# Three raw weight buffers, exchange DMAs ahead of the block's store, and raw loads issued by ScalarE, in the attention stage of a fused block

## The chip, the cores and the metric

The kernel runs on one core of a Trainium2 chip. A core has TensorE (matmuls into PSUM), VectorE, ScalarE, GpSimd (POOL) and SyncE (SP), and 16 DMA engines that all of its DMA queues share. The metric is the device time of one execution in microseconds; the median of several runs counts.

## The reference, cut to what matters

One transformer block on x of 4 x 512 x 1024, in float32: a sequence mixer, a latent cross attention against a context of 4 x 1601 rows, and a feed-forward net whose int32 weights are dequantized. Layer norms stand between them.

```
x = layernorm(x + mixer(x))
C_q = x @ Wq_d ; C_kv = ctx @ Wkv_d                   # latents of 128 and 64
scores[h] = (C_q @ W_qk)[h] @ C_kv.T / 8              # 16 heads, 512 queries, 1601 keys, for each of 4 batches
out[h] = softmax(scores[h]) @ (C_kv @ Wv_u)[h]
x = layernorm(x + out)
w = (w_int - zero) * scale                            # for gate, up (1024 x 3584) and down (3584 x 1024)
x = layernorm(x + (silu(x @ gate) * (x @ up)) @ down)
```

## The kernel before

The program is three functions: `mixer`, `attention` and `ffn`. Each writes out by hand one order of instructions for each engine, and the engines meet at semaphores. This change lies in `attention` and at its borders.

**The work of the attention stage.** It has 256 units: 4 batches x 16 heads x 4 blocks of 128 queries. Two units make a pair (`p` = 0 to 127, 32 pairs for a batch). For a unit, TensorE makes the scores in two halves (L1021), VectorE takes the maximum of each half (L1185, L1196), ScalarE takes the exponents of both (L1107) into `pr`. The half that the code calls 1 has one PSUM place alone, so TensorE makes that half of unit u only when ScalarE has taken the exponents of that half of unit u - 1. VectorE turns most of `pr` in 32 x 32 blocks into `tn` (L1203), TensorE turns the rest (L1050), ScalarE keeps that (L1114). The 32-row blocks of `tn` must then change partitions on their way into `pt`: of the 16 block positions of a pair, 9 go by DMA from SP (L914, "the exchange"), 5 by GpSimd (L1319), 2 by ScalarE (L1122, `cross`). Then TensorE weighs the latents with it (L1040, 26 matmuls a pair) three pairs later. `tn` has two buffers, `pt` three, so the first turn of pair p + 2 on VectorE waits until all 16 pieces of pair p have arrived (`moved`).

**The weights that are prepared beside it.** The feed-forward net wants `w_int - zero` as float32. There are 84 blocks of 128 x 1024 (`BLOCKS`). Each is loaded into `rw` (L921), its zero points into `rz` (L924, a row read into all 128 partitions), GpSimd subtracts (L1370) and casts in place (L1372), and SP stores it to DRAM (L929). There are two buffers of each. Of the 32 pairs of a batch 21 carry a block; the pairs n = 1, 2, 5, 9, 13, 17, 21, 23, 25, 29, 31 of a batch (`FREE`) carry none.

**SP's order.** SP has no other work than to issue DMAs, in this order for each pair:

```
store(block_of(p - 1))      # waits for GpSimd's cast of that block
exchange(p)                 # waits for VectorE's turn of pair p; 9 DMAs
load(block_of(p) + 1)       # waits for the store of the block two before it to land
load_keys / store_rows / load_rows
```

Ahead of pair 0 it issues the keys of batch 1, the load of block 0 and eight loads of rows of x for batches 0 and 1 (L943, 512 KB each). In the last batch it also starts the feed-forward net's first two weight loads (L1533) behind pairs n = 2 and 3, rows for it from n = 28 on (L1540), and at the very end waits for all stores and loads the last rows and the identity (L1574), which TensorE's first step of the feed-forward net waits for (L1637). ScalarE issues DMAs in the mixer alone (L534, 16 stores of 512 KB).

**GpSimd's order.** For each pair: its five pieces, small sums, the output's addition, then `prepare` of the pair's block, then for some pairs a step of the layer norm of the batch before, or the split of the queries (L1326, L1328).

Of the kernel before, what the change touches and what calls it, by code (L numbers as in the profile page):

```python
# [4 lines left out]
F32 = mybir.dt.float32  # L5
F32R = mybir.dt.float32r
I32 = mybir.dt.int32
# [61 lines left out]
def mixer(nc, d, ctxT, wkv_in, wqd_in, wqk_in, wv_in, kvd, cq, ident, shared, x1):  # L69

    with ExitStack() as ctx:
# [8 lines left out]
        first, small, small_late = sem("first"), sem("small"), sem("small_late")  # L80
        xin = [sem(f"xin{k}") for k in range(L + 1)]
        xres, stored = [sem(f"xres{k}") for k in range(RING)], [sem(f"out{k}") for k in range(RING)]
        s_down, s_gelu, s_xmid = sem("down"), sem("gelu"), sem("xmid")
        s_gates, s_prep = sem("gates"), sem("prep")
        s_z, s_sz, s_dt = sem("z"), sem("sz"), sem("dt")
        s_soft, s_e1, s_decay_in = sem("softplus_decay"), sem("e1"), sem("decay_in")
# [7 lines left out]
        s_wctx, s_cin, s_cmm, s_cev = sem("wkv"), [sem(f"cin{k}") for k in range(CXR)], sem("ctx_mm"), sem("ctx_evicted")  # L94
        s_back, s_xT, s_lat, s_cq = (sem(n) for n in ("back", "xT", "latent", "cq"))
        s_kvout = [sem(f"kv_out{k}") for k in range(2)]
        s_early, s_kin, s_pad, s_cnp, s_cn = (sem(n) for n in ("early", "keys_in", "pad", "cn_ps", "cn"))
# [67 lines left out]
        def sync():  # L165
            for dst, src in ((wd, d["wd"]), (bd, d["bd"])):
                Q.dma_start(dst[:], src).then_inc(first, 16)
# [19 lines left out]
            Q.dma_start(wkv[:, :, :], wkv_in[:, :, 0:LAT]).then_inc(s_wctx, 16)  # L187
            Q.dma_start(wqd[:, :, :], wqd_in).then_inc(s_wctx, 16)
# [19 lines left out]
            for dst, src in ((keys["wqk"], wqk_in), (keys["wv"], wv_in)):  # L208
                Q.dma_start(dst, src).then_inc(s_early, 16)
# [12 lines left out]
            Q.wait_ge(s_early, 32)  # L222

        def tensor():
            T.wait_ge(first, 32)
            for l in range(L):
                T.wait_ge(xin[l + 1 if l else 0], 16)
# [73 lines left out]
            def project_out(i, n):  # L301
# [3 lines left out]
                elif n == 0:  # L305
                    T.wait_ge(s_prep, 3)
# [4 lines left out]
            for i in range(2):  # L311
# [5 lines left out]
                if i == 0:  # L317
                    T.wait_ge(s_prep, 2)
# [5 lines left out]
                T.wait_ge(s_wctx, 32)  # L324
# [78 lines left out]
        def scalar():  # L403
            S.wait_ge(first, 32)
            for l in range(L):
                S.wait_ge(s_down, l + 1)
                S.activation(u[:, l * NB:(l + 1) * NB], ps[4 + l][:, :], ACT.Gelu, bias=bd[:, :]).then_inc(s_gelu, 1)
                if l == 1:
                    S.wait_ge(small, 10 * 16)
                    S.wait_ge(s_prep, 1)  # L410
                    S.activation(alog[:, :], alog[:, :], ACT.Exp).then_inc(s_gates, 1)
                    S.activation(g1[:, :], g1[:, :], ACT.Sigmoid).then_inc(s_gates, 1)
            S.wait_ge(s_xmid, L)
# [7 lines left out]
            for i in range(2):  # L421
# [9 lines left out]
                def softplus_and_decay(between):  # L431
                    S.wait_ge(s_dt, (i + 1) * NT)
                    S.activation(E, X, ACT.Abs).then_inc(s_soft, 1)
                    S.wait_ge(s_soft, 4 * i + 1)
                    S.activation(E, E, ACT.Exp, scale=-1.0).then_inc(s_soft, 1)
                    S.wait_ge(s_e1, i + 1)
                    S.activation(R, U1, ACT.Ln).then_inc(s_soft, 1)
                    between()
                    S.wait_ge(s_decay_in, i + 1)
# [126 lines left out]
        def vector():  # L566
# [7 lines left out]
            def keep_input(l):  # L574
                V.wait_ge(s_gelu, l + 1)
                V.tensor_copy(xmid[:, l * NB:(l + 1) * NB], u[:, l * NB:(l + 1) * NB]).then_inc(s_xmid, 1)
# [19 lines left out]
            V.wait_ge(s_gates, 1)  # L596
# [1383 lines left out]
```

## Time and profile before

| | us |
|---|---|
| median of 3 runs | 2720.79 (2718.92 to 2731.97) |
| the profiled execution, whole | 2725.14 |
| its span, first to last instruction | 2721.3 |
| attention, from the first turn to the feed-forward net's first matmul | some 330 to 1412 |

In the profile L12 is line 12 of the kernel, and SPq or ACTq is the sequencer of SyncE or ScalarE that issues a DMA. A group of instructions has a busy time and the idle time of its engine just ahead of it with what ended that. TensorE is the busiest engine over the span, with a clock granted at 0.987 of full speed.

### The profile page before, as it was taken

What the parts mean: (1) busy time and instruction counts of PE and PEld (TensorE: products, weight loads), DVE (VectorE), ACT (ScalarE), POOL (GpSimd) and SP (SyncE); (2) the same over time, 40 slices, a digit from 0 to 9 for tenths busy, and PEclk for the clock granted to TensorE, in tenths of its full rate; (3) what the DMA queues carried; (4) which work ended last, traced back from release to release, by engine and by line L of the source; (5) the groups of instructions that cost most, each with busy time, mean ns of one, the idle gap of its engine ahead of it and who ended that gap; (6) DMA issues with size and microseconds to landing.
All of it is one profiled execution on the core that took longest, in us unless ns stands there. A gap on an engine that the chain in (4) does not pass through costs nothing.

```text
span 2721.3 us, 42088 instructions
## 1 busy us (share of the span) xinstructions
PE 2598.3 (95%) x14328; PEld 1982.2 (73%) x14328; DVE 2274.3 (84%) x2602; ACT 1651.3 (61%) x2588; POOL 2078.3 (76%) x1597
## 2 busy tenths in 40 slices
PE   7998899999999999999988999999999999999997
PEld 4665667777666766676666888888888888788885
DVE  2765688888988898899857999899998899899988
ACT  3454587887777777787755554444455555555553
POOL 1002389889898989888957999999887888888883
PEclk9899999999999999999989999999999999999999
DMA  7426677877777677877772222222213222232222
GB/s 278 167 92 202 213 216 229 231 221 205 230 235 243 203 229 224 246 222 230 223 242 79 100 93 86 70 71 77 76 64 124 78 85 78 70 120 81 79 93 77
DMA packets 166792, 420.64 MB, mean 155 GB/s; under 512 B 30130, under 2 KB 57652, under 8 KB 166068
## 3 DMA queue, kind: packets, MB, share of 16 engines
q1 hardware_dynamic: 164276, 409.57, 48.2%
q10 hardware_dynamic: 2304, 8.39, 0.8%
q8 instruction: 115, 1.88, 0.3%
q14 instruction: 97, 0.79, 0.1%
HBM read 248.43 MB, written 75.04 MB: 119 GB/s over the span
## 4 chain that ended last, share of the span: by engine, by line
PE 48%; POOL 5%; SPq 4%; ACT 2%; DVE 2%; issue 2%; DMA 1%; POOLq 0%; ACTq 0%; DVEq 0%
PE c_ps L1625 43%; SPq L914 3%; PE b_po L1040 2%; PE b_sc L1021 2%; POOL b_pt L1319 1%; POOL b_rw L1370 1%; PE c_ps L1637 1%; POOL shared L1319 1%; ACT b_pr L1107 1%; PE b_mi L1050 0%; POOL b_rw L1372 0%; DVE c_sum_g L1781 0%; POOL b_qs L1328 0%; DVE c_stats L1841 0%; POOL c_sum_g L1866 0%
## 5 line engine op out<-in xcount | busy, mean ns | idle before, releaser
L1781 DVE SCALAR_TENSOR_TENSOR c_acc<-c_ps,c_sd,c_acc 128x1024 f32<-128x1024 f32 x440 | 562.7, 1281 | 92.3 <-PE c_ps L1625 91.6
L1683 ACT ACTIVATE c_scaled<-c_ps,c_sgu 128x1024 f32<-128x1024 f32 x336 | 375.1, 1117 | 422.1 <-PE c_ps L1625 417.5
L1107 ACT ACTIVATE b_pr<-b_sc,b_nm 128x799 f32<-128x799 f32 (+1 forms) x512 | 477.1, 933 | 176.5 <-DVE b_pr L1196 158.1
L1866 POOL TENSOR_TENSOR c_sum_u<-c_sum_u,c_scaled 128x1024 f32<-128x1024 f32 x168 | 404.5, 2408 | 100.4 <-ACT c_scaled L1683 98.9
L1866 POOL TENSOR_TENSOR c_sum_g<-c_sum_g,c_scaled 128x1024 f32<-128x1024 f32 x168 | 404.7, 2409 | 72.7 <-ACT c_scaled L1683 71.7
L1021 PE MATMUL b_sc<-b_kh,b_qs 128*128 128x402 f32 (+1 forms) x1024 | 397.1, 388 | 35.9 <-ACT b_pr L1107 29.7
L1203 DVE STREAM_TRANSPOSE b_tn<-b_pr 128x1280 f32<-128x1280 f32 x256 | 385.4, 1506 | 39.0 <-DMA b_pt<-b_tn 12.3
L1021 PE MATMUL b_sc<-b_kl,b_qs 128*128 128x402 f32 (+1 forms) x1024 | 356.1, 348 | 0.0
L1319 POOL COPY b_pt<-b_tn 32x640 f32<-32x640 f32 x430 | 306.8, 713 | 53.2 <-DVE b_tn L1203 23.6
L1781 DVE SCALAR_TENSOR_TENSOR c_sum_g<-c_ps,c_sgu,c_sum_g 128x1024 f32<-128x1024 f32 x224 | 286.2, 1278 | 25.6 <-PE c_ps L1625 20.0
L1185 DVE TENSOR_REDUCE b_nm_first<-b_sc 128x1 f32<-128x802 f32 x256 | 250.9, 980 | 63.9 <-PE b_sc L1021 60.2
L1196 DVE TENSOR_SCALAR_CACHE_REDUCE b_pr<-b_sc,b_nm_first 128x799 f32<-128x799 f32 x256 | 268.6, 1049 | 30.0 <-PE b_sc L1021 9.4
L1781 DVE SCALAR_TENSOR_TENSOR c_sum_u<-c_ps,c_sgu,c_sum_u 128x1024 f32<-128x1024 f32 x224 | 285.6, 1275 | 6.5 <-POOL c_sum_u L1866 4.3
L1625 PE MATMUL c_ps<-c_hh,c_dw_int 128*128 128x512 f32 x896 | 277.6, 391 | 11.3 <-POOL c_hl L1882 7.1
L1625 PE MATMUL c_ps<-c_xh,c_gw_int 128*128 128x512 f32 x896 | 279.5, 393 | 5.3 <-DVE c_sum_u L1781 3.9
L1625 PE MATMUL c_ps<-c_xh,c_uw_int 128*128 128x512 f32 x896 | 280.0, 394 | 3.0 <-DVE c_xl L1786 1.8
L1625 PE MATMUL c_ps<-c_xl,c_uw_int 128*128 128x512 f32 x896 | 277.0, 390 | 0.0
L1625 PE MATMUL c_ps<-c_xl,c_gw_int 128*128 128x512 f32 x896 | 277.0, 390 | 0.0
L1625 PE MATMUL c_ps<-c_hl,c_dw_int 128*128 128x512 f32 x896 | 276.6, 390 | 0.0
L1021 PEld LDWEIGHTS b_sc<-b_kh,b_qs 128*128 128x128 f32 x1024 | 193.7, 189 | 103.2 <-ACT b_pr L1107 58.4
L1040 PE MATMUL b_po<-b_pt,shared 128*64 128x256 f32 x1720 | 258.9, 389 | 1.8 <-DMA b_pt<-b_tn 1.0
L764 POOL TENSOR_TENSOR a_xt<-a_xt,a_bup 128x1024 f32<-128x1024 f32 x16 | 37.6, 2354 | 263.8 <-DMA a_xt<-in_a_x 207.7
(215 smaller groups left out, 4930.4 us busy)
## 6 DMA issues: line engine op xcount, KB each, us to landing
b_pt<-b_tn SPq DMA_DIRECT2D x774, 80.0 KB, 2.8
shared<-b_tn SPq DMA_DIRECT2D x378, 80.0 KB, 2.7
c_uw_int<-wint_u SPq DMA_DIRECT2D x56, 512.0 KB, 3.5
c_gw_int<-wint_g SPq DMA_DIRECT2D x56, 512.0 KB, 3.4
c_dw_int<-wint_d SPq DMA_DIRECT2D x56, 512.0 KB, 3.4
a_cx<-in_b_ctxT SPq DMA_DIRECT2D x16, 1608.0 KB, 10.0
b_rw<-in_c_gw SPq DMA_DIRECT2D x28, 512.0 KB, 4.2
b_rz<-in_c_gz SPq DMA_DIRECT2D x28, 512.0 KB, 5.6
```

The source lines that it names most:

```text
L914: Q.dma_start(pt[p % MOVES][32 * c:32 * c + 32, a, :, :].rearrange("p t e -> p (t e)"), tn[s][32 * a:32 * a + 32, c, :, :].rearrange("p t ...
L1021: ins = T.matmul(sc[:, at:at + n], qs[g // 2 % 2][:, g % 2, q * P:(q + 1) * P], k[b % 2][:, k0:k0 + n], start=(z == 0), stop=(z == 1))
L1040: ins = T.matmul(po[z * LAT:(z + 1) * LAT, s * 256:(s + 1) * 256], cn[:, b, t, :], turned, start=(t < 2), stop=(t >= NKT - 2))
L1107: S.activation(pr[u % 2][:, k0:k1], sc[:, at + lo:at + hi], ACT.Exp, bias=nm[:, u % 2:u % 2 + 1], accum_out=den[:, g % 2, q, half:half + 1 ...
L1185: V.tensor_reduce(nm0[:, u % 2:u % 2 + 1], sc[:, at + SIDE[0][0]:at + SIDE[0][1]], AX, ALU.max, negate=True).then_inc(s_part, 1)
L1196: V.tensor_scalar(pr[u % 2][:, SIDE[1][2]:SIDE[1][3]], sc[:, at + SIDE[1][0]:at + SIDE[1][1]], -1.0, nm0[:, j], ALU.mult, ALU.min, accum_o ...
L1203: V.transpose(tn[u // 2 % 2][:, :, u % 2, :], pr[u % 2][:, 0:4 * SEG].rearrange("p (c e) -> p c e", c=4)).then_inc(s_tt, 1)
L1319: G.tensor_copy(pt[p % MOVES][32 * c:32 * c + 32, a, :, :], tn[s][32 * a:32 * a + 32, c, :, :]).then_inc(s_block, 1)
L1625: ins = T.matmul(pair[slot % 4][:, b * 512:(b + 1) * 512], w[n][t % 2][:, k * P:(k + 1) * P], v[:, b * 512:(b + 1) * 512], start=(z == 0), ...
L1683: S.activation(dst[:, :], pair[SLOT[x, t] % 4][:, :], ACT.Identity, scale=scale(x, t)).then_inc(s_e, 1)
L1781: V.scalar_tensor_tensor(out=total, in0=pair[SLOT[x, t] % 4][:, :], scalar=scale(x, t), in1=before, op0=ALU.mult, op1=ALU.add).then_inc(s_ ...
L1866: G.tensor_tensor(total, total, scaled[m % 2][:, :], ALU.add).then_inc(s_add, 1)
```

## The change

It has five parts in the attention stage, and some in names of semaphores.

1. `RAW = 3`: three buffers of `rw` and of `rz`. The new first one lies in the tensor `shared`, behind the keys and the kept queries.
2. SP issues `exchange(p)` ahead of `store(block_of(p - 1))`.
3. SP loads blocks 0, 1 and 2 ahead of pair 0. ScalarE issues the load of every later block, block i + 3 behind `cross` of two pairs after block i's, once the store of block i has landed.
4. The keys of batches 2 and 3 are loaded in two halves behind two pairs, and not both behind one.
5. The feed-forward net's first two weight loads move from n = 2 and 3 of the last batch to n = 29 and 30, behind a wait for the stores out of the first raw buffer.

In the mixer and the attention stage several semaphores are merged into one with counts to match: each wait still names the same instruction (or one that comes no earlier than what was waited for), so no order changes there.

```diff
-KEYS_LOAD = {24: 2, 52: 3}
+KEYS_LOAD = {24: (2, 0), 25: (2, 1), 52: (3, 0), 53: (3, 1)}
+RAW = 3
...
-        rw = [sb(f"b_rw{j}", [P, HID], I32) for j in range(2)]
-        rz = [sb(f"b_rz{j}", [P, HID], I32) for j in range(2)]
+        rw = [sb(f"b_rw{j}", [P, HID], I32) for j in range(RAW - 1)]
+        rz = [sb(f"b_rz{j}", [P, HID], I32) for j in range(RAW - 1)]
+        raw_at = keys_end + NB
+        rw.insert(0, shared[:, raw_at:raw_at + HID].bitcast(I32))
+        rz.insert(0, shared[:, raw_at + HID:raw_at + 2 * HID].bitcast(I32))
...
             Q.wait_ge(s_kl0, 2)
-            load_keys(1)
-            load(0)
+            for z in range(2):
+                load_keys(1, z)
+            for i in range(RAW):
+                load_first(i)
...
             def pair(p):
+                exchange(p)
                 if p and block_of(p - 1) is not None:
                     store(block_of(p - 1))
-                exchange(p)
-                i = block_of(p)
-                if i is not None and i + 1 < len(BLOCKS):
-                    load(i + 1)
...
+            def load(i):                                  # ScalarE
+                n, j = BLOCKS[i]
+                S.wait_ge(s_wout[i % RAW], 16 * (i // RAW))
+                S.dma_start(rw[i % RAW][:, :], raw[n + "w"][j, :, :]).then_inc(s_rin[i % RAW], 16)
+                S.wait_ge(s_sub, i - RAW + 1)
+                S.dma_start(rz[i % RAW][:, :], raw[n + "z"][j:j + 1, :].broadcast_to([P, HID])).then_inc(s_rin[i % RAW], 16)
...
                 if k % 2 and 3 <= k < 2 * PAIRS + 3:
                     cross((k - 3) // 2)
+                    i = block_of((k - 3) // 2 - 2) if k >= 7 else None
+                    if i is not None and i + RAW < len(BLOCKS):
+                        load(i + RAW)
...
+FIRST_PAIR = 29
...
-                if 2 <= n < 2 + len(FIRST):
-                    load(*FIRST[n - 2])
+                if FIRST_PAIR <= n < FIRST_PAIR + len(FIRST):
+                    Q.wait_ge(b['wout'][0], 16 * len(BLOCKS) // RAW)
+                    load(*FIRST[n - FIRST_PAIR])
```

## Rows read from the trace of the kernel before

**Rows 1.** The page, busy time of the engines over the span.

```profile
PE 2598.3 (95%) x14328; PEld 1982.2 (73%) x14328; DVE 2274.3 (84%) x2602; ACT 1651.3 (61%) x2588; POOL 2078.3 (76%) x1597
```

**Rows 2.** Windows, weighing matmuls (L1040) alone: stretch, length, PE, PEld, clock, DMA.

```profile
378.80:411.10 32.30, 13.79 (x106) 7.24 (x106) 1.00 0.83 237
773.80:810.60 36.80, 14.29 (x106) 7.36 (x106) 0.95 0.78 228
843.30:879.30 36.00, 13.83 (x106) 7.27 (x106) 1.00 0.86 262
1114.80:1150.50 35.70, 13.84 (x106) 7.30 (x106) 1.00 0.87 263
1314.20:1352.20 38.00, 14.21 (x105) 7.43 (x105) 0.96 0.67 206
345.90:1383.90 1038.00, 429.49 (x3226) 225.64 (x3226) 1.00 0.76 226
```

**Rows 3.** The exchange's DMAs, their landing and who waited for them (us, times).

```profile
  DVE b_tn L1203: 19.7, 15
...
DMA to landing us min/median/max: 2.0/2.8/8.2
```

**Rows 4.** Timeline of SP's queue, 1093 to 1113 us.

```profile
1094.29 7.78 SPq L914 DMA_DIRECT2D b_pt<-b_tn  x9
...
1103.70 0.43 SPq L929 DMA_DIRECT2D wint_g<-b_rw  x1
1104.23 6.10 SPq L914 DMA_DIRECT2D shared<-b_tn  x9
1112.31 0.34 SPq L921 DMA_DIRECT2D b_rw<-in_c_dw  x1
```

**Rows 5.** Timeline of VectorE, the turns of the same stretch.

```profile
1098.00 1.51 DVE L1203 STREAM_TRANSPOSE b_tn<-b_pr 128x1280 f32<-128x1280 f32 x1
...
1114.84 1.51 DVE L1203 STREAM_TRANSPOSE b_tn<-b_pr 128x1280 f32<-128x1280 f32 x1 [4.10 <-issue]
```

**Rows 6.** Waits of SP's queue, whole span: waited for, us, times, longest.

```profile
SPq L929 <- POOL b_rw L1372: 53.6, 41, 4.5
```

**Rows 7.** Timeline of SP's queue and of VectorE about the start of the stage.

```profile
324.26 3.75 SPq L943 DMA_DIRECT2D b_y<-x  x8
334.48 5.65 SPq L914 DMA_DIRECT2D b_pt<-b_tn  x9
...
345.41 1.51 DVE L1203 STREAM_TRANSPOSE b_tn<-b_pr 128x1280 f32<-128x1280 f32 x1 [1.80 <-ACT b_pr L1107]
```

**Rows 8.** DMA view, 326 to 342 us: traffic in 40 slices, GB/s.

```profile
GB/s 240 168 170 205 276 410 410 379 420 389 369 399 410 410 410 399 430 410 410 410 410 420 399 430 399 410 420 410 410 399 420 399 420 410 410 368 261 187 224 224
```

**Rows 9.** ScalarE's DMA issues in the mixer.

```profile
L534 ACTq DMA_DIRECT2D x<-a_xt x16: 326/362/369, 246.8 to 310.3; - x16
```

**Rows 10.** Where ScalarE's sequencer stood ahead of `cross`, and ScalarE's and TensorE's timelines behind it.

```profile
L1120 ACTq EVENT_SEMAPHORE  x1: 17/17/17, 410.5 to 410.5; - x1
...
411.23 1.47 ACT L1122 COPY b_pt<-b_tn 32x640 f32<-32x640 f32 x2
412.72 0.93 ACT L1107 ACTIVATE b_pr<-b_sc,b_nm 128x799 f32<-128x799 f32 x1
...
414.09 0.35 PE L1021 MATMUL b_sc<-b_kh,b_qs 128*128 128x402 f32 x1
```

**Rows 11.** The turn that the store's place hangs on, and the store's landing.

```profile
395.62 1.50 DVE L1203 STREAM_TRANSPOSE b_tn<-b_pr 128x1280 f32<-128x1280 f32 x1
...
DMA to landing us min/median/max: 2.8/6.4/10.0
```

**Rows 12.** The stage's end: SP's queue, and TensorE's wait.

```profile
1402.64 2.71 SPq L1540 DMA_DIRECT2D c_xs<-x  x5
1405.39 0.43 SPq L1574 DMA_DIRECT2D c_ident<-in_ident  x1
...
PE c_ps L1637 <- DMA c_ident<-in_ident: 2.7, 1, 2.7
```

More of the change, by code:

```diff
@@ L78, in mixer @@
         T, V, S, G, Q = nc.tensor, nc.vector, nc.scalar, nc.gpsimd, nc.sync
-        first, small, small_late = sem("first"), sem("small"), sem("small_late")
+        small, small_late = sem("small"), sem("small_late")
         xin = [sem(f"xin{k}") for k in range(L + 1)]
         xres, stored = [sem(f"xres{k}") for k in range(RING)], [sem(f"out{k}") for k in range(RING)]
-        s_down, s_gelu, s_xmid = sem("down"), sem("gelu"), sem("xmid")
-        s_gates, s_prep = sem("gates"), sem("prep")
+        s_down, s_gelu = sem("down"), sem("gelu")
+        s_prep = sem("prep")
         s_z, s_sz, s_dt = sem("z"), sem("sz"), sem("dt")
-        s_soft, s_e1, s_decay_in = sem("softplus_decay"), sem("e1"), sem("decay_in")
+        s_soft, s_soft_in = sem("softplus_decay"), sem("softplus_decay_in")
         s_x, s_xc, s_tr, s_xst, s_fcd = (sem(n) for n in ("x", "xc", "tr", "xst", "fcd"))
@@ L92, in mixer @@
         s_mix, s_bup, s_up, s_res, s_var, s_std, s_nmr, s_out = (sem(n) for n in ("mix", "bup_in", "up", "res", "var", "std", "nmr", "normalised"))
-        s_wctx, s_cin, s_cmm, s_cev = sem("wkv"), [sem(f"cin{k}") for k in range(CXR)], sem("ctx_mm"), sem("ctx_evicted")
+        s_wts, s_cin, s_cmm, s_cev = sem("attention_weights"), [sem(f"cin{k}") for k in range(CXR)], sem("ctx_mm"), sem("ctx_evicted")
         s_back, s_xT, s_lat, s_cq = (sem(n) for n in ("back", "xT", "latent", "cq"))
         s_kvout = [sem(f"kv_out{k}") for k in range(2)]
-        s_early, s_kin, s_pad, s_cnp, s_cn = (sem(n) for n in ("early", "keys_in", "pad", "cn_ps", "cn"))
+        s_kin, s_pad, s_cnp, s_cn = (sem(n) for n in ("keys_in", "pad", "cn_ps", "cn"))
         wd = sb("a_wd", [P, KC, DM])
@@ L166, in sync @@
             for dst, src in ((wd, d["wd"]), (bd, d["bd"])):
-                Q.dma_start(dst[:], src).then_inc(first, 16)
+                Q.dma_start(dst[:], src).then_inc(xin[0], 16)
             for z in range(2):
@@ L221, in sync @@
                 Q.wait_ge(s_kvout[k], 4 * 4 * 16)
-            Q.wait_ge(s_early, 32)
+            Q.wait_ge(s_wts, 64)
         def tensor():
-            T.wait_ge(first, 32)
             for l in range(L):
-                T.wait_ge(xin[l + 1 if l else 0], 16)
+                T.wait_ge(xin[l + 1 if l else 0], 16 if l else 48)
                 for c in range(KC):
@@ L409, in scalar @@
                     S.wait_ge(small, 10 * 16)
[L410 to L413, printed above, removed]
+                    S.wait_ge(s_prep, 3)
+                    S.activation(alog[:, :], alog[:, :], ACT.Exp).then_inc(s_soft, 1)
+                    S.activation(g1[:, :], g1[:, :], ACT.Sigmoid).then_inc(s_soft, 1)
+            S.wait_ge(s_prep, 6)
             def keep_context(pair):
@@ L845, in attention @@
         s_root = sem("root")
-        s_rin, s_sub, s_cast = [sem("raw0"), sem("raw1")], sem("sub"), sem("cast")
-        s_wout = [sem("wint0"), sem("wint1")]
+        s_rin, s_sub, s_cast = [sem(f"raw{j}") for j in range(RAW)], sem("sub"), sem("cast")
+        s_wout = [sem(f"wint{j}") for j in range(RAW)]
         keys = keys_of(shared)
@@ L943, in load_rows, with load_keys @@
                 Q.dma_start(y[b % 2][:, q, :], x1_v[b, :, q, :]).then_inc(yin[b % 2], 16)
-            def load_keys(b):
-                for z in range(2):
-                    Q.dma_start(kv[z * LAT:(z + 1) * LAT, 0:NKV], kvd[b, :, :]).then_inc(kin[b], 16)
+            def load_keys(b, z):
+                Q.dma_start(kv[z * LAT:(z + 1) * LAT, 0:NKV], kvd[b, :, :]).then_inc(kin[b], 16)
             Q.wait_ge(s_kl0, 2)
-            load_keys(1)
-            load(0)
+            for z in range(2):
+                load_keys(1, z)
+            for i in range(RAW):
+                load_first(i)
             for b in range(2):
@@ L1568, in early @@
                 if p == PAIRS - 1:
-                    for k in range(2):
-                        Q.wait_ge(b['wout'][k], 16 * len(BLOCKS) // 2)
+                    for k in range(RAW):
+                        Q.wait_ge(b['wout'][k], 16 * len(BLOCKS) // RAW)
                     for t in range(QT, HT):
```

68 lines of the change are left out of this document (32 added, 36 removed).

## The prediction, made before the result

> **What bounds the kernel now.** I read the page first. TensorE is busy 95% of the span [rows 1], VectorE 84%, GpSimd 76%. The change lies in the attention stage, about 1080 of 2721 us, so the question is how far TensorE is from its own pace there, and who holds it up.
>
> The windows over the weighing matmuls answer the first half [rows 2]. The work repeats every four pairs, and a pair weighs with 26 matmuls, so I cut windows from one pair's first weighing matmul to that of the fourth pair behind it (104; a window also counts one or two that it cuts). An undisturbed window takes 32.3 us. The whole of pairs 0 to 123 is 31 such windows and takes 1038.0 us, where 31 x 32.3 = 1001.3. So TensorE loses 37 us in all. Some 7 us of it are real matmuls, the turning of three batches' latents, which sit in a few pairs alone: I leave them. Some 29 us are stalls. They are in clumps: the four disturbed windows shown are 36.8, 36.0, 35.7 and 38.0 us long, 17.3 us over four quiet ones.
>
> Who causes the clumps? The view of the exchange's DMAs gives VectorE's turn 15 waits and 19.7 us for their landing [rows 3], and the timelines show how one comes about [rows 4, 5]. VectorE's second turn of pair 92 ended at 1098.00 + 1.51 = 1099.5. SP was still issuing pair 91's exchange (from 1094.29, 7.78 us), then a load, rows, the store of block 60 at 1103.70, and only then, at 1104.23, pair 92's exchange, 4.7 us behind its turn. It was issued by 1110.3, landed some 4 us later, and VectorE's turn started at 1114.84 after 4.10 us of idleness. The next load waited until 1112.31 for a store to land, and the next exchange stood behind it in the queue. The waits of SP's queue give the other half: 41 waits, 53.6 us, of the store for GpSimd's cast [rows 6]; the exchange stands behind each. So in the clumps the bound is SP's order: TensorE waits for exponents, these for VectorE, VectorE for an exchange that was issued late.
>
> **The change part by part.**
>
> *The exchange ahead of the store, and no load in SP's queue.* The exchange of a pair can now start when its turn ends. SP then has 9 issues of some 0.63 us (5.65 in all where nothing crowds them [rows 7], 7.78 at worst in the rows shown) and one store of 0.3 to 0.4, under the 8.1 us of a pair, so it doesn't fall behind. In the example the exchange would be issued at about 1099.5 in place of 1104.23, 4.7 us earlier, where VectorE's wait is 4.10. Bounds: nothing comes back if the landing is held by traffic (below); all 29 us if every stall is of this kind. I take the 17.3 us of the shown clumps and 4 us for the small ones like them, 21 us; the other 8 I leave, since VectorE's own added work (statistics and variance of the layer norm) sits in some of them.
>
> *Three buffers.* GpSimd's subtraction no longer waits for zero points. GpSimd isn't what TensorE waits for, so it gives nothing by itself. But its work doesn't shrink, and where the layer norm's steps are added it runs later than its turn pair by pair; if that cover went, VectorE would wait for GpSimd's five pieces. I charge nothing, and keep a few us for it in the range.
>
> *The first three loads.* Two more blocks go ahead of the rows and of pair 0's exchange, which is issued at 334.48 [rows 7] into a queue already full: the DMA engines move about 410 GB/s from 330 to 341 us [rows 8]. Two blocks are four DMAs of 512 KB; at 410 GB/s that is 4 x 1.28 = 5.1 us. VectorE's turn of pair 2 stood idle 1.80 us for that exchange already [rows 7], so all of the 5.1 us is on the path: +5 us. Lower bound 4 (some of it was paid by the load that the old order put between pairs 0 and 1), upper 6.5, if the broadcast rows are slower than plain ones.
>
> *The load on ScalarE.* In the mixer a 512 KB issue by ScalarE takes 0.36 us [rows 9]; two are 0.7 us. Where do they fall? Behind `cross`, and right behind it is the exponent of half 1. An example: `cross` of pair 9 runs from 411.23 for 1.47 us, the exponent from 412.72 for 0.93, and TensorE's scores that need it start at 414.09, 0.44 us behind its end [rows 10]. So on the engine's own time there would be hardly room. But ScalarE's sequencer was already at the wait ahead of `cross` at 410.5, 2.2 us before that exponent: with a wait that is fulfilled the two issues fit under work already handed to the engine. Cost nothing. The two ends: 0, and 0.7 - 0.44, about 0.3 us, for each of 81 loads, 24 us, if the lead can't be used. I take 1 us in all, near the first end, as the row at 410.5 shows the lead itself.
>
> The load's wait is nearer. It needs the store two pairs back to have landed. In the same example that is block 4: pair 8's turn ends at 395.62 + 1.50 = 397.1 [rows 11], its exchange would be issued by 402.8 to 404.9, the store 0.4 later, and a store lands 2.8 / 6.4 / 10.0 us (least, median, most) after its issue. That is 406.0, 409.7 or 415.3. ScalarE is there at 410.5 and must be through by 412.72 + 0.44 = 413.2 less 0.7, 412.5. So the median store is in time by 2.8 us and the slowest is late by the same.
>
> At this place a rule of the Trainium skill speaks against the change. "Perfetto Trace Analysis", section "DMA Instruction — HWDGE", has a DMA issue wait for a lock on the one descriptor generator that the issuing sequencers share. By it each of ScalarE's issues could stand behind one of the exchange's (an estimate by that rule: 0.7 + 2 x 0.6 = 1.9 us in place of 0.7), which would use up the lead. The mixer's ScalarE issues took at most 0.369 us [rows 9], so I see no such wait there.
>
> *The keys in halves* moves one issue of 0.5 us by a pair: nothing. *The merged semaphores* order nothing anew: nothing.
>
> *The end.* Now the exchange of pair 127 was issued by 1402.5, behind the last store, five loads of rows by 1405.35, and then the identity, for which TensorE waited at the feed-forward net's start [rows 12]. The last store now comes behind that exchange, and all the rows behind its landing: some 2.5 us more from the exchange's end to the identity. The net's two first weight loads, 1.28 us each, come into the same stretch. Against that the exchanges of pairs 125 to 127 no longer stand behind loads: about -3.5 to -4 us. Together -1 us, between +3 and -3.
>
> **The sum.** -21 + 5 + 1 + 0 - 1 = -16 us. The profiled execution took 2725.1 us, 3.8 more than its span of 2721.3; it becomes 2709. The median of the runs is 2720.8, 4.3 under the profiled execution, so the forecast for the median is 2705 us.
>
> **The rivals.**
>
> *ScalarE waits for the store (slower).* The place is the wait ahead of `load`, on the sequencer that also hands out the exponents. It decides from landings of about 9 us in that example (412.5 less 403.7). For it: a store's worst is 10.0, and clumps have the most traffic (263 GB/s in two windows [rows 2]). Against it: the median of 6.4 was taken with an exchange and a load crowding it. If half of 81 loads are late by 1.3 us, 53 us: 2758 us. A quarter of that is still 2718. Chance of a time over 2734: 0.17.
>
> *The traffic holds the exchange, not the order (no change).* For it: pair 92's exchange landed 4 us after its last issue where the median is 2.8 [rows 3], so DMA engines were backed up there, and the bytes stay the same. Against it: that queue held a load, rows and a store issued just ahead, and its start was 4.7 us late whatever the landing. Then the gain is lost and the start's 5 us and ScalarE's 1 are paid: 2727 us; half of the gain leaves 2716. Chance 0.33 for 2707 to 2734. A rule of the Trainium skill, "DMA: Bandwidth & Descriptors", section "Issuing engines are not separate DMA queues", says the same of moving issues: it saves only the sequencer's time of issuing, and the transfers still share 16 engines. The trace can't show it before the loads are moved.
>
> *More comes back.* All 29 us but 5, and the start at 4: 2697 us, chance 0.1; the forecast itself 0.4.
>
> **How the numbers follow.** A measurement of this kernel tells about 0.5% from no change, 13.6 us: below 2707.2 is faster, above 2734.4 slower. The forecast and the case below it make 0.5 for faster, the traffic's cases 0.33, the first rival 0.17. The likeliest case alone spans 2697 to 2714. The range that holds 8 in 10 runs from 2694 (all stalls gone, the least start) to 2738, which takes in the traffic's cases and the mild end of the slower one.
>
> **What the changed kernel's profile would show.** VectorE's turns wait for exchange landings for under 5 us in place of 19.7. SP's waits for GpSimd's cast nearly go, and an exchange starts within 1 us of its turn. The turn of pair 2 starts 5 us later behind a queue of loads. GpSimd's subtraction waits for nothing. ScalarE's load issues take 0.4 to 0.6 us each; a wait of over 2 us at them, with TensorE's scores waiting for exponents behind it, would be the first rival. Exchanges that start on time and land over 5 us after issue would be the second. The prediction is wrong if the first weighing matmul moves by more than 7 us, or if four-pair windows of 36 us are left.

## The result, and the profile after

| | before | after |
|---|---|---|
| median of 14 runs each, us | 2721.43 (2714.34 to 2731.97) | 2736.19 (2727.97 to 2743.79) |
| profiled execution, us | 2725.14 | 2728.45 |
| its span, us | 2721.3 | 2726.7 |

The ratio is 1.0051, with a 95% interval of 1.0039 to 1.0063: slower by 14.8 us, where 2705 us was forecast. The profiled execution after is a fast one of its kind: of the 14 runs one alone was faster. In a later set of runs the same kernel gave 2727.17 (2718.03 to 2736.02, 12 runs) beside 2723.00 for the kernel before, 1.0016 [1.0002, 1.0029]. A set is run on one chip, and different sets on different ones or at other times; so some 0.3% between sets lies on top of each interval. Both say slower, neither faster, and kernels of one set are the ones to compare closely.

The page after, busy line [rows 1]:

```profile
PE 2599.3 (95%) x14328; PEld 1983.6 (73%) x14328; DVE 2271.5 (83%) x2602; ACT 1652.7 (61%) x2588; POOL 2081.1 (76%) x1597
```

The work is the same. Windows over the weighing matmuls, for the pairs of [rows 2] (52, 60, 92 and 116, each with the three behind it), then pairs 12, 32 and 96, then the whole (stretch, length, PE, PEld, clock, DMA share, GB/s):

```profile
789.50:822.30 32.80, 13.80 (x106) 7.25 (x106) 1.00 0.95 278
855.30:888.00 32.70, 13.78 (x104) 7.22 (x104) 1.00 0.94 267
1121.10:1155.30 34.20, 13.84 (x106) 7.28 (x106) 1.00 0.93 258
1322.30:1355.10 32.80, 13.81 (x106) 7.26 (x106) 1.00 0.83 251
454.20:489.80 35.60, 13.84 (x106) 7.29 (x106) 1.00 0.78 219
619.70:655.90 36.20, 13.79 (x104) 7.23 (x104) 1.00 0.53 144
1155.30:1190.60 35.30, 13.82 (x104) 7.26 (x104) 1.00 0.52 144
352.10:1386.80 1034.70, 430.00 (x3226) 226.07 (x3226) 1.00 0.78 224
```

The old clumps did go: the first four windows fell from 146.5 to 132.5 us together. The granted clock is 1.00 of full speed in all of them, so it plays no part. But other windows grew: pairs 12, 32 and 96 began windows of 34.1, 33.5 and 32.3 us before and of 35.6, 36.2 and 35.3 now. The whole is 3.3 us shorter, where 21 were forecast. And the first weighing matmul comes 22.5 us behind the stage's first turn (352.1 less 329.6) where it was 16.4 (345.9 less 329.5).

Timelines of SP's queue, of ScalarE (its queue, and one exponent) and of VectorE's turns about pair 12, after:

```profile
439.99 5.58 SPq L916 DMA_DIRECT2D b_pt<-b_tn  x9
...
448.25 6.11 SPq L916 DMA_DIRECT2D b_pt<-b_tn  x9
```
```profile
444.43 0.34 ACTq L1130 DMA_DIRECT2D shared<-in_c_gw  x1
444.81 0.51 ACTq L1132 DMA_DIRECT2D shared<-in_c_gz  x1
...
447.23 0.92 ACT L1104 ACTIVATE b_pr<-b_sc,b_nm 128x802 f32<-128x802 f32 x1
```
```profile
438.45 1.51 DVE L1210 STREAM_TRANSPOSE b_tn<-b_pr 128x1280 f32<-128x1280 f32 x1
...
452.88 1.51 DVE L1210 STREAM_TRANSPOSE b_tn<-b_pr 128x1280 f32<-128x1280 f32 x1 [1.84 <-ACT b_pr L1104]
```

Pair 12's second turn ends at 438.45 + 1.51 = 439.96 and its exchange starts at 439.99: on time, as forecast. Its nine pieces are issued by 445.57. At 444.43, 4.4 us into them, ScalarE issues a load of 1 MB. The exchange's DMAs in two stretches, 430.5 to 436.4 us (pair 11, no load issued meanwhile) and 439.9 to 445.6 us (pair 12):

```profile
L916 SPq DMA_DIRECT2D shared<-b_tn x9: 507/591/592, 430.6 to 435.6; - x9
...
DMA to landing us min/median/max: 2.1/2.6/2.9
```
```profile
L916 SPq DMA_DIRECT2D b_pt<-b_tn x9: 508/591/592, 440.0 to 445.0; - x9
...
DMA to landing us min/median/max: 2.0/2.1/7.8
```

The last pieces of pair 12 take up to 7.8 us in place of 2.9: the exchange has landed at 445.0 + 7.8 = 452.8, and the turn of pair 14, which needs that buffer, starts at 452.88. Its row puts the idle time down to "ACT b_pr", but the later of the two exponents that it reads was through by 447.23 + 0.92 = 448.2; what came at 452.8 is the landing. So the view of waits must be read with care here.

The DMA view shows what the last two pieces (issued at 444.34 and 444.97) stood behind. These are the packets that started in three stretches, 445.5 to 447.0, 447.0 to 448.5 and 448.5 to 449.5 us; q1 is SP's queue, q10 ScalarE's (packets, MB, share of the 16 engines):

```profile
q10 hardware_dynamic: 58, 0.24, 85.3%
```
```profile
q10 hardware_dynamic: 109, 0.38, 70.0%
q1 hardware_dynamic: 48, 0.08, 16.2%
```
```profile
q10 hardware_dynamic: 63, 0.26, 72.8%
```

In the first and the last stretch no packet of SP's queue starts, though a piece of the exchange is still outstanding. From the eighth piece's issue to the exchange's landing, SP's queue pauses for 1.7 us at the median in the 82 pairs of the stage whose exchange meets a load, and for over 1 us in 57 of them, each time while packets of ScalarE's queue start; in the 38 pairs without a load it never pauses for more than 0.3 us.

The idle time of VectorE's turns over the stage:

```profile
L1210 DVE STREAM_TRANSPOSE b_tn<-b_pr x256: 1499/1506/1515, 329.6 to 1394.3; 128x1280 f32<-128x1280 f32 x128
its engine sat idle before it (us, times) until:
  ACT b_pr L1104: 25.3, 16
  issue: 24.4, 16
  DMA b_pt<-b_tn: 3.1, 5
```

By its labels the landing of exchanges costs 3.5 us where it was 19.7 [rows 3], and the forecast of "under 5 us" would be right; by its sum the turns are idle for 53.9 us (38.4 before). All of it is the landing: each of the 39 gaps after, and each of the 25 before, ends within 0.1 us of the moment when the last piece of the exchange two pairs back has landed. So the 19.7 us of [rows 3] were half of that wait. I went through the pairs one by one: for each, the latest landing of its nine pieces less the end of its second turn. In 82 of the pairs 4 to 123 ScalarE issued a load in or just about the exchange (3 us ahead of the turn's end to 7.5 behind it; at the median 5.0 behind), and these land 10.8 us behind the turn at the median, 13.5 at worst. The 38 others land at 7.3.

The start, SP's queue and VectorE's turn of pair 2 [rows 7]:

```profile
322.58 0.58 SPq L921 DMA_DIRECT2D shared<-in_c_gw  x1
...
326.29 7.23 SPq L941 DMA_DIRECT2D b_y<-x  x8
334.60 14.04 SPq L916 DMA_DIRECT2D b_pt<-b_tn  x18
```
```profile
352.14 1.51 DVE L1210 STREAM_TRANSPOSE b_tn<-b_pr 128x1280 f32<-128x1280 f32 x1 [8.40 <-issue]
```

ScalarE's issues [rows 9], the raw weights and the zero points of a `d` block, and under each the landing of all 81 of its line:

```profile
L1130 ACTq DMA_DIRECT2D b_rw<-in_c_dw x27: 334/334/353, 393.7 to 1378.8; - x27
...
DMA to landing us min/median/max: 3.8/4.6/8.0
```
```profile
L1132 ACTq DMA_DIRECT2D b_rz<-in_c_dz x27: 444/532/1612, 394.1 to 1379.2; - x27
...
DMA to landing us min/median/max: 4.8/6.5/12.0
```

And the end, TensorE's wait for the identity, 2.7 us before [rows 12]:

```profile
PE c_ps L1646 <- DMA c_ident<-in_ident: 5.3, 1, 5.3
```

### The profile page after: what moved, and what is told of

It reads as the page before. It is cut to its first block, busy times and chain, and to the rows that moved or that the text cites. A ratio compares the mean times of both kernels' runs of the same rounds, so it can differ in the third digit from the quotient of the medians.

```text
span 2726.7 us, 42088 instructions
## 1 busy us (share of the span) xinstructions
PE 2599.3 (95%) x14328; PEld 1983.6 (73%) x14328; DVE 2271.5 (83%) x2602; ACT 1652.7 (61%) x2588; POOL 2081.1 (76%) x1597
## 4 chain that ended last, share of the span: by engine, by line
PE 51%; DVE 5%; SPq 4%; DMA 4%; ACT 3%; POOL 3%; issue 3%; ACTq 0%; POOLq 0%; DVEq 0%
PE c_ps L1634 42%; SPq L916 4%; PE b_sc L1018 3%; PE b_po L1037 3%; DMA b_pt<-b_tn 2%; DVE b_tn L1210 2%; DMA shared<-b_tn 1%; ACT b_pr L1104 1%; DVE b_pr L1203 1%; DVE b_nm_first L1192 1%; PE b_mi L1047 1%; POOL b_pt L1326 1%; PE b_mi L1056 1%; PE c_ps L1646 1%; DVE c_sum_g L1790 1%
## 5 line engine op out<-in xcount | busy, mean ns | idle before, releaser
L1018 PE MATMUL b_sc<-b_kh,b_qs 128*128 128x402 f32 (+1 forms) x1024 | 397.8, 388 | 35.6 <-ACT b_pr L1104 30.3
L1790 DVE SCALAR_TENSOR_TENSOR c_sum_g<-c_ps,c_sgu,c_sum_g 128x1024 f32<-128x1024 f32 x224 | 286.3, 1278 | 25.5 <-PE c_ps L1634 19.7
```

The lines of the kernel that those rows point to most:

```text
L1018: ins = T.matmul(sc[:, at:at + n], qs[g // 2 % 2][:, g % 2, q * P:(q + 1) * P], k[b % 2][:, k0:k0 + n], start=(z == 0), stop=(z == 1))
L1790: V.scalar_tensor_tensor(out=total, in0=pair[SLOT[x, t] % 4][:, :], scalar=scale(x, t), in1=before, op0=ALU.mult, op1=ALU.add).then_inc(s_ ...
```

## The experiments

In the table "start" is the time from the stage's first turn to the first weighing matmul, "pace" that from the latter to the first weighing matmul of pair 124, and "late" the number of exchanges of pairs 3 to 123 that land over 11 us behind their turn, all from the profiled execution. Times and ratios are of all runs; rows between two lines of dashes are one set, run on one chip with the kernel before.

```
                                            median  ratio to before          start  pace  late
before                                      2721.4                            16.4 1038.0  29
after                                       2736.2  1.0051 [1.0039, 1.0063]   22.5 1034.7  39
-----
e1  loads by SP behind exchange and store   2712.4  0.9968 [0.9957, 0.9979]   20.9 1021.0   7
e2  blocks 1, 2 behind exchanges 0, 1       2725.3  1.0006 [0.9991, 1.0022]   16.4 1041.5  46
e3  ScalarE's load one exponent later       2708.4  0.9953 [0.9941, 0.9965]   22.1 1018.0   1
e4  before + exchange ahead of store        2738.8  1.0063 [1.0048, 1.0077]   16.5 1046.6  35
-----
e5  e1 + e2                                 2706.4  0.9934 [0.9913, 0.9955]   16.4 1019.6   7
e6  zero points as plain rows               2725.5  1.0010 [0.9994, 1.0026]   22.3 1032.8  39
e7  e3 + e2                                 2700.6  0.9918 [0.9898, 0.9939]   16.5 1016.5   1
e8  ScalarE's load one exponent earlier     2732.3  1.0036 [1.0023, 1.0050]   21.6 1043.3  51
-----
e9  after, once more                        2727.2  1.0016 [1.0002, 1.0029]   21.7 1031.6  35
e10 e7, store ahead of the exchange         2718.0  0.9979 [0.9966, 0.9993]   16.4 1031.3  21
-----
e11 e3 once more                            2707.0  0.9945 [0.9933, 0.9957]   22.0 1018.6   1
e12 e7 once more                            2701.7  0.9930 [0.9913, 0.9947]   16.4 1016.0   0
```

### e1: the loads back in SP's queue, behind the exchange and the store

```diff
             def pair(p):
                 exchange(p)
                 if p and block_of(p - 1) is not None:
                     store(block_of(p - 1))
+                i = block_of(p - 2) if p >= 2 else None
+                if i is not None and i + RAW < len(BLOCKS):
+                    load(i + RAW)             # the same two DMAs, issued by SP; none on ScalarE
```

> The changed kernel with one thing undone: the loads of raw blocks are issued by SP again, behind the exchange and the store of the pair two behind the block's (exchange, store, load), with three buffers; the first three loads stay where the change put them. Theory A (the load collides with the exchange: ScalarE issued it some 4.5 us into an exchange's 5.6 us of issuing, and the exchange's last pieces then land together with it): every exchange lands 7 to 8 us after its turn instead of 10 to 13, VectorE's turns wait for almost none, the middle loses some 10 to 20 us, 2712 to 2722 us, ratio to the kernel before 0.995 to 1.000, with the start's 6 us still paid. Theory B (traffic as such: the same bytes hold the exchange wherever the loads stand in time): exchanges still land 10 to 13 us after the turn in pairs with traffic, ratio 1.003 to 1.007 as the changed kernel. Theory C (issuing on ScalarE costs ScalarE's own time): as theory A in time, but the exchange landings of the changed kernel's sort stay.

2712.4 us, 0.9968. The same bytes in the same buffers; the load now starts when all nine pieces are issued. Seven exchanges are late in place of 39 and the pace is 13.7 us better. The time of the load decides, not that it is made.

### e2: blocks 1 and 2 out of the start

```diff
-            for i in range(RAW):
-                load_first(i)
+            load_first(0)
...
                 exchange(p)
+                if p < RAW - 1:
+                    load_first(p + 1)
```

> The changed kernel with only block 0 loaded ahead of the rows and pair 0; blocks 1 and 2 are loaded behind the exchanges of pairs 0 and 1. All theories: the first weighing matmul comes back from 352.1 to about 346 us, and the kernel gains 5 to 6 us on the changed one, ratio to the kernel before 1.002 to 1.004. If the start's delay is hidden later it gains nothing, ratio 1.005.

The start is back at 16.4 us: all 6.1 us of its loss were the two blocks ahead of the rows. Of the pace nothing came back (1041.5), with 46 late exchanges: the median, 2725.3, is the level of the kernel before, and the ratio is better than the 1.002 to 1.004 of the expectation. How much of the step from 2736.2 is the start and how much the other set of runs, this run alone can't tell; e11 and e12 do.

### e3: ScalarE's load one exponent later

```diff
+                i = block_of((k - 8) // 2) if k % 2 == 0 and 8 <= k < NU else None
+                if i is not None and i + RAW < len(BLOCKS):
+                    load(i + RAW)             # now behind exponent(k, 1) of the next unit
...
                     cross((k - 3) // 2)
-                    i = block_of((k - 3) // 2 - 2) if k >= 7 else None
-                    if i is not None and i + RAW < len(BLOCKS):
-                        load(i + RAW)
```

> The changed kernel with ScalarE's load issued one exponent later (behind the exponent of half 1 of the next unit), so some 2 us later, about 6.5 us after the turn of the running exchange, when its 5.6 us of issuing are over. Theory A: exchanges land 7 to 8 us after their turn in most pairs, and the time falls by 8 to 15 us against the changed kernel, ratio to the kernel before 0.999 to 1.003. Theory B: landings and time as in the changed kernel, ratio 1.004 to 1.007. Theory C: the issues still stand in ScalarE's queue, now with an exponent queued behind them, ratio 1.004 to 1.010.

2708.4 us, 0.9953, better than any theory gave: by the ratios 27 us under the changed kernel's first set and 17 under its second, with the same loads, from the same queue, some 2 us later. The same load as above (that of block 9) in this kernel's timelines of SP's and ScalarE's queues, and the landing of pair 12's exchange:

```profile
436.50 5.57 SPq L916 DMA_DIRECT2D b_pt<-b_tn  x9
...
445.61 5.62 SPq L916 DMA_DIRECT2D b_pt<-b_tn  x9
```
```profile
443.67 0.34 ACTq L1130 DMA_DIRECT2D shared<-in_c_gw  x1
```
```profile
DMA to landing us min/median/max: 2.0/2.1/2.1
```

The load starts 1.6 us behind the last piece of pair 12 (issued by 442.07), whose pieces all land in 2.0 to 2.1 us, and 1.9 us ahead of pair 13's. Over the stage it starts 1.3 us ahead of a turn's end at the median. It then shares the engines with the first pieces of the next exchange, and that exchange lands 7.8 us behind the turn at the median (7.4 in the ten pairs that meet no load): first pieces that come late cost little, since the buffer waits for the last one.

### e4: the kernel before, with the exchange ahead of the store alone

```diff
-                if p and block_of(p - 1) is not None:
-                    store(block_of(p - 1))
                 exchange(p)
+                if p and block_of(p - 1) is not None:
+                    store(block_of(p - 1))
```

> The kernel before with one part of the change alone: the exchange ahead of the store, still two buffers and loads by SP. The load that follows in the same pair needs the store just issued to land (3 to 6 us), and SP stands at it. Theory of SP's order: a pair with blocks on both sides takes SP 5.6 + 0.4 + 4 + 1.1 = 11 us of the 8.1 us of a pair, so the clumps grow, ratio 1.01 to 1.03. If only the late start of the exchange mattered, ratio 0.993 to 0.997.

2738.8 us, 1.0063. With two buffers the load behind must wait for the store issued just ahead of it, and the next exchange stands behind both. Waits of SP's queue in this kernel:

```profile
SPq L921 <- DMA wint_g<-b_rw: 54.8, 20, 5.2
...
SPq L921 <- DMA wint_u<-b_rw: 51.8, 20, 4.5
```

So the order alone is a loss. That it is the third buffer which mends it is shown by e1, which has the same order, three buffers and the other parts of the change: its loads are SP's too, and none waits for a store.

### e5: e1 and e2 together

The edits of e1 and e2 in one kernel.

> All loads in SP's queue, behind the exchange and the store of their pair, three buffers, and blocks 1 and 2 behind the exchanges of pairs 0 and 1. With the loads in SP's queue but all three ahead of the rows it was 2712.4 us and its first weighing matmul at 351.3. Theory (start and loads add): 6 us less, about 2706 to 2707, ratio 0.9945 to 0.995, turns' idle gaps some 7 us. Rival (the start only moves): 2712, ratio 0.997.

2706.4 us, 0.9934, start 16.4, pace 1019.6: the two add. The median of ScalarE's queue at the right time (e7, same set) is 5.8 us better, 3.1 of them in the pace, but with six runs each the two intervals overlap, so the difference is likely and not shown. The profiles would have a reason for it: in SP's queue the loads still make exchanges start late, 22.0 us summed over the pairs, where e7 has none.

### e6: the zero points as plain rows

This kernel subtracts the weights from themselves: the load of zero points reads 128 rows of the weights in place of one row 128 times.

```diff
-                S.dma_start(rz[i % RAW][:, :], raw[n + "z"][j:j + 1, :].broadcast_to([P, HID])).then_inc(s_rin[i % RAW], 16)
+                S.dma_start(rz[i % RAW][:, :], raw[n + "w"][j, :, :]).then_inc(s_rin[i % RAW], 16)
```

> The changed kernel, but the load of the zero points reads 512 KB of distinct rows of the weights in place of one 4 KB row read into 128 partitions, from ScalarE's queue at the same places (this changes the computation: weights are subtracted from themselves). Same bytes written, other source. Theory 1 (the broadcast read is slow, and holds the DMA engines longer than its bytes): the load lands in under 5 us, exchanges that land over 11 us after their turn fall from 39 to under 20, and the time falls to about 2720 or less. Theory 2 (any megabyte issued into the running exchange does it): exchanges as late as in the changed kernel, 35 to 42 of them over 11 us, time 2732 to 2740, ratio 1.004 to 1.007.

39 late exchanges, as in the changed kernel, pace 1032.8 beside its 1034.7 and 1031.6. The time, 1.0010, lies a little under what theory 2 expected, and about the changed kernel's second ratio of 1.0016. The broadcast read isn't the cause, as its landing shows too, 6.5 us at the median in both kernels; any megabyte at that moment does it.

### e7: e3 and e2 together

The edits of e3 and e2 in one kernel.

> The changed kernel with both repairs: ScalarE's load is issued behind the next exponent of half 1 (some 2 us later, as in the run with that alone, 2708.4 us, first weighing matmul at 351.4 us), and blocks 1 and 2 are loaded behind the exchanges of pairs 0 and 1 and not ahead of the rows. Theory (the two causes are separate and add): the first weighing matmul comes back to about 345.5 us, the turns' idle gaps for landings stay under 5 us over the stage, and the time is about 5 to 6 us under the one with the late load alone: 2703 us, ratio to the kernel before 0.993 to 0.994. Rival (the start's loads only move, and crowd the next exchanges, so that the 6 us are lost again in later pairs, as with the early load): about 2708, ratio 0.995.

2700.6 us, 0.9918, 20.5 us under the kernel before in its set and 2.4 us better than expected. Windows over the weighing matmuls, for the pairs 52, 92, 116, 32 and 96 and the whole:

```profile
769.30:802.00 32.70, 13.79 (x105) 7.22 (x106) 1.00 0.91 268
...
1097.60:1130.00 32.40, 13.87 (x106) 7.32 (x106) 1.00 0.90 271
1293.60:1326.40 32.80, 13.83 (x106) 7.27 (x106) 1.00 0.84 247
...
603.40:636.90 33.50, 13.83 (x104) 7.28 (x104) 1.00 0.55 154
1130.00:1162.30 32.30, 13.80 (x105) 7.24 (x106) 1.00 0.54 155
341.50:1358.00 1016.50, 428.62 (x3224) 225.45 (x3224) 1.00 0.77 231
```

That of pair 96 carries as many bytes as in the kernel after in 3.0 us less. The turns are idle for 2.8 us in the stage, and no more:

```profile
its engine sat idle before it (us, times) until:
  ACT b_pr L1105: 2.2, 1
  issue: 0.6, 2
```

### e8: ScalarE's load one exponent earlier

```diff
                     exponent(k, 1)
+                i = block_of((k - 7) // 2) if k % 2 and 7 <= k < NU else None
+                if i is not None and i + RAW < len(BLOCKS):
+                    load(i + RAW)             # and none behind cross
```

> The changed kernel with ScalarE's load issued about 2 us earlier (behind the exponent of half 1 of the same unit, ahead of cross), some 2 to 2.5 us into the exchange in place of 4.4 to 5. Theory (a load whose megabyte is in the DMA engines while the exchange's pieces come behind it delays them; the more pieces come behind it, the more): exchanges still land 10 to 13 us behind the turn, turns' idle gaps 45 us or more, time 2736 to 2745, ratio 1.005 to 1.009. Rival (only the last pieces matter, those issued in the same microsecond as the load; a load that early drains before the last pieces come): landings fall back to 8 to 9 us, time about 2715 to 2720.

2732.3 us, 1.0036, pace 1043.3, 51 late exchanges: those with a load (now issued 3.2 us behind the turn's end at the median) land at 11.1 us. The rival fell. But half of the theory's reading fell too: the turns are idle for 24.8 us, 17.3 of them behind the start, not 45, and the time is under the 2736 that it gave. The new loss is elsewhere. ScalarE's timeline, both of its queue and of the engine:

```profile
457.54 0.93 ACT L1104 ACTIVATE b_pr<-b_sc,b_nm 128x799 f32<-128x799 f32 x1 [0.98 <-DVE b_pr L1203]
...
458.63 0.34 ACTq L1130 DMA_DIRECT2D b_rw<-in_c_dw  x1
459.01 1.30 ACTq L1132 DMA_DIRECT2D b_rz<-in_c_dz  x1
460.37 0.93 ACT L1104 ACTIVATE b_pr<-b_sc,b_nm 128x802 f32<-128x802 f32 x1 [1.80 <-issue]
```

Right behind that exponent the sequencer has no lead over its engine: the engine stands idle for both issues, 1.80 us. Such idle time ("issue" ahead of exponents and of the kept output) is 36.9 us in 38 places, beside 0.2 us at the exponents of the changed kernel in the stage. This is the price that the prediction bounded at 0.3 us a load and took as nothing; behind `cross` it is nothing, one place earlier it is not.

### e9: the changed kernel once more

> The changed kernel itself once more, for a second profile: its first profiled execution was 2728.5 us, 8 us under its own median of 2736.2, while that of before was 4 us over its own, so the two profiles show only a third of the difference of the medians. Expected if the rest is spread of where loads meet exchanges: a profile of 2730 to 2740 us with more pairs whose exchange lands over 11 us behind the turn than the 39 of the first, and turns idle for more than 46.5 us. Expected if it lies outside the stage: the same 35 to 42 pairs and 46 us, and the first weighing matmul or the feed-forward net later by some us.

2727.2 us, profiled at 2728.0. The stage is like the first profile's (35 late exchanges, turns idle for 46.9 us, pace 1031.6, start 21.7). The first guess, more late exchanges, is refuted; of the second the counts fit, but nothing outside the stage came later either (feed-forward net 1311.4 us for 1311.7), and the time lies 9 us under the first median. What lies between the two sets I can't say.

### e10: e7 with the store ahead of the exchange

```diff
             def pair(p):
+                if p and block_of(p - 1) is not None:
+                    store(block_of(p - 1))
                 exchange(p)
                 if p < RAW - 1:
                     load_first(p + 1)
-                if p and block_of(p - 1) is not None:
-                    store(block_of(p - 1))
```

> The best kernel so far (2700.6 us: ScalarE's load one exponent later, blocks 1 and 2 behind the exchanges of pairs 0 and 1), with one part of the change undone: SP issues the store ahead of the exchange again. Three buffers and loads on ScalarE stay. Theory 1 (the store's wait for GpSimd's cast is what made exchanges late in the kernel before; with three buffers GpSimd is not held by zero points, but its work is as long): SP waits for casts again, exchanges start up to 3 us late in pairs with a block, their sum over 20 us, turns idle for 10 us or more, time 2706 to 2714. Theory 2 (three buffers alone end those waits, as GpSimd is then early): the store's wait is under 5 us over the stage, time 2699 to 2703.

2718.0 us, 0.9979, 14.8 us slower in the pace than e7, more than either theory gave. SP waits for casts again:

```profile
SPq L927 <- POOL b_rw L1380: 77.8, 50, 4.3
...
SPq L927 <- POOL shared L1380: 60.1, 27, 6.4
```

Not all of it delays an exchange (late starts sum to 69 us), but an exchange that starts late runs again into the load that ScalarE issues in its own order: 21 are late, and the turns are idle for 29.0 us. That is how I read the excess over the theory; no run parts the two. Exchange first is worth about 15 us, once the loads are out of its way.

### e11 and e12: e3 and e7 in one set

> The kernel with ScalarE's load one exponent later and the three first loads still ahead of the rows, once more, on the same chip as the one with both repairs: the pair tells what the start alone costs at the end of the run, free of the difference between chips (the changed kernel itself gave ratios of 1.0051 and 1.0016 on two of them). Theory (the start's 6 us reach the end undiminished): 2707 to 2711, ratio 0.9950 to 0.9965, 5 to 7 us over the kernel with both repairs.

> The kernel with both repairs once more, beside the one with the late load alone. Theory (the start's 6 us reach the end undiminished): 2701 to 2705, ratio 0.992 to 0.9945, 5 to 7 us under its neighbour. Rival (a part is lost in later pairs): within 3 us of its neighbour.

2707.0 and 2701.7 us. The start's loads cost 5.3 us at the end of the run, 5.6 from the first turn to the first weighing matmul. e7's ratio is 0.9930 [0.9913, 0.9947] here.

## Why the prediction was wrong

**The step that failed** is the term of -21 us, "the exchange ahead of the store, and no load in SP's queue". What it rested on was right: that the stalls come from exchanges issued late, that the order in SP's queue causes it, and how much could come back. Exchanges now start on time (0.6 us late in sum over pairs 3 to 123, 182 before, starts within 0.05 us not counted), the four shown clumps gave 14.0 of their 17.3 us, and in e7, where nothing else was put in the way, the pace improves by 1038.0 - 1016.5 = 21.5 us. Wrong was to treat the load as gone once it had left SP's queue. It went to ScalarE's, behind `cross`, and that place is fixed to the same turn that starts the exchange: 5.0 us behind it at the median, when the last pieces are being issued. Those make the landing 3.5 us later at the median (10.8 for 7.3) all along the stage, in place of late starts in clumps. The pace gave 3.3 us (6.4 in e9). The prediction priced ScalarE's issues, on the engine and on the sequencer, and its wait for the store, but not where in the exchange a megabyte would start.

**The range** of 2694 to 2738 us holds 2736.2, but not by merit: its upper part was there for traffic and for waits of ScalarE for the store, and the forecast went the other way. A time over 2734 had a chance of 0.17 for that second cause, which did not occur. Of the two signs of being wrong that it named, the first weighing matmul moved by 6.2 us, under its 7, but one window of 36.2 us is left, that of pair 32 (33.5 before): by the second sign it was wrong. One sum is off in itself: for "more comes back", -24, +4, +1 and -1 give 2701 us, not 2697.

**The start**, +5 us with 4 and 6.5 as its ends: 6.1 in the profile, 5.3 at the end of the run (e11 less e12). Right in mechanism, and nearly in size: the turn of pair 2 is idle for 8.40 us where it was 1.80.

**The load on ScalarE**, +1 us: right for this place. Its raw issues take 0.33 to 0.38 us, those of the zero points 0.33 to 1.61 (0.4 to 0.6 were forecast), and neither shows as idle time of exponents. e8 shows that the other end, the lost lead, is real. By the rule of the Trainium skill on the lock of the one descriptor generator ("Perfetto Trace Analysis", section "DMA Instruction — HWDGE") they should have stood behind exchange issues: at 444.43, in the midst of SP's nine, the issue took 0.34 us and SP's pieces kept their 0.591. Of the 81 raw issues 80 overlap an issue of SP, and none took over 0.38 us, so no such wait is seen there. Of the two zero-point issues over 1 us, the one of 1.61 us overlaps an issue of SP that is long too (1.70 us), the other, 1.37 us at 798.09, overlaps none; what makes them long stays open.

**Three buffers**, nothing: right, GpSimd's subtraction has no wait any more. **The end**, -1 us between +3 and -3: the identity comes later, a wait of 5.3 us for 2.7, and from the first weighing matmul of pair 124 to the net's first matmul it takes 28.2 us for 28.0: +0.2.

**The rivals.** ScalarE waiting for the store: no such wait in the kernel after; a bit of it appears in e8 (12.4 us for landed stores, in 9 places). The traffic: its time, 2727 us, is the nearest of all, and its mark, exchanges that start on time and land late, is what the profile shows. But not for its reason. It said that the bytes hold the landing wherever they are issued; e1, e3 and e7 move the same bytes, in e7 at 231 GB/s for 224, and land at 7.6 to 7.8 us at the median over all pairs, where the kernel after lands at 10.0. That transfers on another engine's queue share the 16 DMA engines, so that moving an issue saves only the sequencer's time (the Trainium skill, "DMA: Bandwidth & Descriptors", section "Issuing engines are not separate DMA queues"), holds in these traces. What decided is another thing: moving the issue also moved the transfer in time, here onto the last pieces of the one series whose landing was waited for.

**The sum and what stays open.** Of the profiles: start +6.1, pace -3.3, end of the stage +0.2, and the feed-forward net +2.3 (1311.7 us for 1309.4, no instruction of it changed) come to +5.3; the rest is rounding and the stretch ahead of the stage. The net's 2.3 us are no effect that is shown: over the fourteen profiles of this record it took 1307.5 to 1313.3 us. The profiled execution of the kernel after, 2728.45, lies 7.0 us over the median of before, and the medians differ by 14.8 in the one set and by 4.2 in the other. What put the first set's runs some 8 us over their profile stays open. That the overlap in time is what delays the pieces is shown by e1, e3 and e8, and the packets show SP's queue standing meanwhile; why it pauses for as long as 1.7 us at a time stays open.

## What to carry to other kernels

A DMA moved to another engine's queue is moved in time too: ask which small DMA's landing the path waits for, and in which microsecond of it the moved one will start. Where one large transfer must share the engines with a series of small ones, start it right behind the last piece, where it meets only the first pieces of the next series: the changed kernel with only ScalarE's load one exponent later and blocks 1 and 2 loaded behind the exchanges of pairs 0 and 1 is 0.7 to 0.8% faster than the kernel before, where the change as made is 0.2 to 0.5% slower. And sum the idle time of the waiting engine, not only the rows labelled with the suspect: here the label fell from 19.7 to 3.5 us while the idle time rose from 38.4 to 53.9. That sum tells where to look, not what it costs: of the rise 6.6 us are the start, and behind the start the turns were idle for 45.5 us in place of 36.6 while the pace was still 3.3 us shorter. Against e7, with 0.6 us there, 36.6 us of idleness went with 21.5 us of pace before, and 45.5 with 18.2 after.

## What the runs showed of the hardware that was not expected

- A piece of the exchange (80 KB) lands 2.1 to 2.9 us behind its issue where no load is beside it (pair 11), and 7.8 us behind it where 1 MB starts in the midst of the series (the last piece of pair 12; at most 8.0 in pairs 4 to 123). Behind the three blocks and the rows of the start it took up to 12.4 us (pair 0).
- While packets of ScalarE's load ran, SP's queue started none for 1.7 us at the median of the 82 pairs with a load, though a piece of it was outstanding; without a load its longest pause was 0.3 us.
- A DMA issue on ScalarE's queue costs its engine nothing where the sequencer has a lead, and 1.80 us for two issues where it has none, in the same kernel's order one exponent apart.
- A row of 4 KB read into 128 partitions is no slower than 128 rows: issued behind another load of 512 KB, both land 6.5 us behind their issue at the median (at worst 12.0 and 10.4).
- One kernel's ratio to another's differed by 0.35% between two sets of runs, with intervals of 0.12 to 0.14% to either side.
